# Splitting the gathered rows into two halves, and summing them by two single-pass products

## The reference

```
messages = jnp.einsum('ei,oi->eo', x[col], W) + b
out = jax.ops.segment_sum(messages * agg_weight, row, num_segments=x.shape[0])
x = _layernorm(x + out, axis=-1)
```

## Time and profile before

| | us |
|---|---|
| median of 3 runs (range) | 1298.23 (1295.89 to 1300.33) |
| the profiled execution, its own time | 1291.46 |
| its span, first to last instruction | 1289.7 |
| busy: PE / DVE / ACT / POOL | 962.8 / 756.4 / 650.0 / 577.0 |
| mean granted clock of PE | 0.855 of full |
| sorting part, up to the first step of the second part | about 358 |

### The profile page before, as it was taken

The page is one execution under the profiler, slowest core; times in us unless marked ns, Lnnn a source line. Parts: engine busy times, 40 slices in busy tenths (PEclk is TensorE's granted clock), DMA queues, the critical chain, the costliest instruction groups (busy, mean ns, idle before and its releaser), DMA issues.

```text
span 1289.7 us, 22501 instructions
## 1 busy us (share of the span) xinstructions
PE 962.8 (75%) x7063; PEld 745.4 (58%) x7063; DVE 756.4 (59%) x3474; ACT 650.0 (50%) x1658; POOL 577.0 (45%) x610
## 2 busy tenths in 40 slices
PE   5776877777752676787778777887778777877786
PEld 4543444444432666666667666676667566766676
DVE  7865656566642555566555655565556555655577
ACT  0344444444411464565556555565566555655568
POOL 2344445454454534544454445544544445444520
PEclk9889989889875878898898888877898888887888
DMA  2111111111031444444455445544454445444543
GB/s 68 34 51 34 51 34 51 34 50 48 19 104 41 146 128 139 152 157 138 143 166 155 139 142 151 163 135 138 152 161 141 135 152 167 143 133 143 166 136 136
DMA packets 80818, 147.63 MB, mean 114 GB/s; under 512 B 19152, under 2 KB 20188, under 8 KB 80700
## 3 DMA queue, kind: packets, MB, share of 16 engines
q1 hardware_dynamic: 62076, 117.10, 27.3%
q0 software_dynamic: 18624, 29.08, 8.8%
HBM read 94.19 MB, written 51.93 MB: 113 GB/s over the span
## 4 chain that ended last, share of the span: by engine, by line
PE 42%; DVE 21%; another core or an unknown queue 20%; issue 11%; ACT 5%; DMA 0%; ACTq 0%; POOL 0%; SPq 0%; DVEq 0%; POOLq 0%
PE bank L663 12%; PE bank L681 10%; PE bank L618 8%; DVE stats L946 5%; DVE sel L933 4%; DVE h L940 3%; PE bank L669 3%; DVE mv L952 2%; PE bank L554 2%; PE bank L684 2%; PE bank L573 2%; ACT same_hi L983 2%; PE bank L570 1%; ACT y L1035 1%
## 5 line engine op out<-in xcount | busy, mean ns | idle before, releaser
L507 POOL DMA_INDIRECT xg<-in_x,now x441 | 423.3, 960 | 471.5 <-DVE now L925 338.5
L663 PE MATMUL bank<-sel,xg 128*128 128x308 f32 (+11 forms) x1370 | 359.0, 395 | 80.2 <-issue 69.3
L940 DVE SCALAR_TENSOR_TENSOR h<-bank,aw,xt 128x512 f32<-128x512 f32 x196 | 146.4, 747 | 387.6 <-remote 349.7
L663 PEld LDWEIGHTS bank<-sel,xg 128*128 128x128 f32 x1370 | 264.4, 221 | 142.9 <-issue 114.3
L681 PE MATMUL bank<-wT,aggT 128*128 128x128 f32 x1568 | 263.1, 315 | 103.2 <-issue 69.8
L1035 ACT ACTIVATE y<-h,shift,rstd 128x128 f32<-128x128 f32 x784 | 320.2, 480 | 0.0
L681 PEld LDWEIGHTS bank<-wT,aggT 128*128 128x128 f32 x1568 | 228.0, 219 | 133.7 <-issue 88.3
L1022 ACT COPY aggT<-bank 128x512 f32<-128x512 f32 x196 | 111.9, 571 | 321.0 <-remote 255.7
L470 POOL DMA_INDIRECT place_scratch<-word_col,place_row x141 | 140.6, 997 | 159.7 <-DVE place_row L824 113.6
L946 DVE BATCH_NORM_STATS2 stats<-h 128x6 f32<-128x128 f32 x784 | 169.2, 278 | 0.2
L933 DVE TENSOR_SCALAR sel<-iota_win,now 128x308 f32<-128x308 f32 (+1 forms) x441 | 144.5, 375 | 0.0
(11 more groups left out here) (145 smaller groups left out, 772.5 us busy)
## 6 DMA issues: line engine op xcount, KB each, us to landing
xt<-in_x SPq DMA_DIRECT2D x195, 256.0 KB
out<-y SPq DMA_DIRECT2D x195, 256.0 KB
hi_row<-hi_scratch SPq DMA_DIRECT2D x25, 512.0 KB
xg<-in_x,now POOLq DMA_INDIRECT x441
place_scratch<-word_col,place_row POOLq DMA_INDIRECT x141
place_scratch<-scattered SPq DMA_DIRECT2D x1, 441.0 KB, 6.3
scattered<-place_scratch SPq DMA_DIRECT2D x1, 441.0 KB, 3.2
src_rows<-in_src SPq DMA_DIRECT2D x1, 192.0 KB
```

The costliest lines, as they stand in the source:

```text
L507: nc.gpsimd.indirect_dma_start(out=xg[:, m, k], out_offset=None, in_=x, in_offset=bass.IndirectOffsetOnAxis(ap=now[:, m, k, 0:1], axis=0)) ...
L663: last = nc.tensor.matmul(sums[:, nodes], xg[:, ring, k], sel[:, half, k, cols], start=(i == 0), stop=(i == len(lists) - 1), skip_group_ch ...
L940: V.scalar_tensor_tensor(h[:, u].rearrange("p j d -> p (j d)"), OUT[u % RO][:], aw[:], xt[:, u].rearrange("p j d -> p (j d)"), ALU.mult, A ...
```

## The change

The product of a list is no longer made in float32. The gathered rows are cut by DVE into an upper part, in which the lowest 12 bits of each number are cleared (`cut`), and the rest, `xg - cut` (`xl`). ACT copies the upper part into a buffer of type float32r (`xh`). `xl` and `sel` have this type too. For each product of before, PE makes two, `xh` by `sel` and `xl` by `sel`, into the same sums; float32r is the 32-bit type that PE takes in a single pass. In the trace of before, a float32 product is two instructions, so that the number of instructions on PE stays the same for these sums.

DVE now does two more instructions in each round, one over the 128 to 384 columns of the group's lists on a single source (`cut`), and one on two sources (`xl`), and waits for the gathers there. PE waits no longer for the gathers but for DVE and ACT. ACT has one more copy in each round, ahead of `keep_sums`, whose lag and those of the later stages grow by three. The windows now begin and end at even nodes, so that two of the nine selection matrices are 310 wide. The sorting buffers of the first part have moved into a space that the second part uses again.

```diff
-        sel = sb("sel", [P, 2, LISTS, SW])
+        sel = sb("sel", [P, 2, LISTS, SW], f32r)
+        xh = sb("xh", [P, 2, LISTS, D], f32r)
+        xl = sb("xl", [P, 2, LISTS, D], f32r)
+        cut = sb("cut", [P, 2, LISTS, D])
...
-                    if u % SPAN_G == 0:
-                        pe.wait_ge(s_first[m], 16 * mn + 16)
-                    pe.wait_ge(s_rest[m][u % SPAN_G], (16 * mn + 16) * len([k for k in CLASS[u % SPAN_G] if k]))
+                    pe.wait_ge(s_upper, min(g + 2, GA) if u % SPAN_G == SPAN_G - 1 else g + 1)
+                    pe.wait_ge(s_lower, min(g + 2, GA) if u % SPAN_G == SPAN_G - 1 else g + 1)
...
-                        last = nc.tensor.matmul(sums[:, nodes], xg[:, ring, k], sel[:, half, k, cols],
-                                                start=(i == 0), stop=(i == len(lists) - 1), skip_group_check=True)
+                    for i, (half, k, cols, nodes) in enumerate(lists):
+                        nc.tensor.matmul(sums[:, nodes], xh[:, half, k], sel[:, half, k, cols],
+                                         start=(i == 0), stop=False, skip_group_check=True)
+                        last = nc.tensor.matmul(sums[:, nodes], xl[:, half, k], sel[:, half, k, cols],
+                                                start=False, stop=(i == len(lists) - 1), skip_group_check=True)
...
-                    for k in CLASS[u % SPAN_G]:
+                    mine = CLASS[u % SPAN_G]
+                    lists = slice(mine[0], mine[-1] + 1)
+                    if u % SPAN_G == 0:
+                        dve.wait_ge(s_first[m], 16 * mn + 16)
+                    dve.wait_ge(s_rest[m][u % SPAN_G], (16 * mn + 16) * len([k for k in mine if k]))
+                    V.tensor_scalar(cut[:, m % 2, lists].bitcast(i32), xg[:, m, lists].bitcast(i32), 12, 12, LSR, LSL
+                                    ).then_inc(s_cut, 1)
+                    for k in mine:
                         V.tensor_scalar(sel[:, m % 2, k, 0:WIDTH[k]], iota_win[:, WIN[k]:WIN[k] + WIDTH[k]],
                                         now[:, m, k, 1:2], None, ALU.is_equal).then_inc(s_sel, 1)
+                    dve.wait_ge(s_cut, g + 1)
+                    V.tensor_tensor(xl[:, m % 2, lists], xg[:, m, lists], cut[:, m % 2, lists], ALU.subtract).then_inc(s_lower, 1)
...
+                def keep_upper(g, u, n, period, m, mn):
+                    lists = slice(CLASS[u % SPAN_G][0], CLASS[u % SPAN_G][-1] + 1)
+                    act.wait_ge(s_cut, g + 1)
+                    nc.scalar.copy(xh[:, m % 2, lists], cut[:, m % 2, lists]).then_inc(s_upper, 1)
...
-                rounds([(keep_sums, 0), (spread_of, 3), (normalise, 4)])
+                rounds([(keep_upper, 0), (keep_sums, 3), (spread_of, 6), (normalise, 7)])
```

More of the change, by code:

```diff
@@ L18, in gnn_resnorm_kernel @@
     f32, i32 = mybir.dt.float32, mybir.dt.int32
-    bf16, f16 = mybir.dt.bfloat16, mybir.dt.float16
+    bf16, f16, f32r = mybir.dt.bfloat16, mybir.dt.float16, mybir.dt.float32r
     ALU, ACT, AX = mybir.AluOpType, mybir.ActivationFunctionType, mybir.AxisListType.X
@@ L34, in gnn_resnorm_kernel @@
     FIRST = [-(-SPAN_N * k // LISTS) for k in range(LISTS + 1)]
-    WIN = [(FIRST[k] - TAIL) % GN for k in range(LISTS)]
-    WIDTH = [FIRST[k + 1] - FIRST[k] + TAIL for k in range(LISTS)]
-    SW = max(WIDTH) + max(WIDTH) % 2
+    START = [(FIRST[k] - TAIL) // 2 * 2 for k in range(LISTS + 1)]
+    WIN = [START[k] % GN for k in range(LISTS)]
+    WIDTH = [FIRST[k + 1] + FIRST[k + 1] % 2 - START[k] for k in range(LISTS)]
+    SW = max(WIDTH)
     TAIL_FROM = SPAN_N - LISTS * TAIL
-    CLASS = [[k for k in range(LISTS) if max(FIRST[k] - TAIL, 0) // GN == u] for u in range(SPAN_G)]
+    CLASS = [[k for k in range(LISTS) if max(START[k], 0) // GN == u] for u in range(SPAN_G)]
     PARTS = []
@@ L43, in gnn_resnorm_kernel @@
         for k in range(LISTS + 1):
-            start = FIRST[k] - TAIL
+            start = START[k]
             lo, hi = max(start, u * GN), min(start + WIDTH[k % LISTS], (u + 1) * GN)
@@ L168, in sort_sb @@
                 return sorting.enter_context(nc.sbuf_tensor(name, shape, dt))
+            src_rows = sort_sb("src_rows", [P, KB, P], i32)
+            dst_rows = sort_sb("dst_rows", [P, KB, P], i32)
+            e0 = sort_sb("e0", [P, KB, P], i32)
+            e1 = sort_sb("e1", [P, KB, P], i32)
+            e2 = sort_sb("e2", [P, KB, P], i32)
+            pos = sort_sb("pos", [P, KB, P], i32)
+            chunk = sort_sb("chunk", [P, KB, P], i32)
+            bucket = sort_sb("bucket", [P, KB, P], i32)
+            word1 = sort_sb("word1", [P, KB, P], i32)
+            word2 = sort_sb("word2", [P, KB, P], i32)
             oh_lo = sort_sb("oh_lo", [P, B, BC // 2, LO, 2], bf16)
@@ L269, in gnn_resnorm_kernel @@
         s_sel = sem("s_sel")
+        s_upper = sem("s_upper")
+        s_lower = sem("s_lower")
+        s_cut = sem("s_cut")
         s_agg = sem("s_agg")
@@ L654, in aggregate @@
                     else:
[L655 to L656 removed]
                         pe.wait_ge(s_sel, LISTS * period + LISTS + 1)
                     sums, counts_of = AGG[q], DEG[g // 2 % 2]
[L659 removed]
+                    lists = [((m + k // LISTS) % 2, k % LISTS, slice(lo, hi), slice(at, at + hi - lo))
                              for k, lo, hi, at in parts]
                     at_least(pe, s_aggc, g - 1)
[L662 to L664 removed]
+                    for i, (half, k, cols, nodes) in enumerate(lists):
[3 more added lines that the diff above has]
+                                                start=False, stop=(i == len(lists) - 1), skip_group_check=True)
                     last.then_inc(s_sum, 1)
@@ L667, in aggregate @@
                         at_least(pe, s_degc, g // 2 - 1)
-                    for i, (ring, half, k, cols, nodes) in enumerate(lists):
+                    for i, (half, k, cols, nodes) in enumerate(lists):
                         last = nc.tensor.matmul(counts_of[:, nodes], ones_deg[:, q], selh[:, half, k, cols],
```

14 lines of the change are left out of this document (removed).

## The result

The changed kernel took 1336.87 us (median of 4, 1332.39 to 1338.16), the kernel before 1297.90 (4, 1295.89 to 1300.33). The ratio is 1.0289, 95% interval 1.0252 to 1.0327: slower by 39 us, where 1414, 116 more, was forecast. The sign was right and the size three times too large.

What follows compares the result with a forecast made beforehand. A period was taken as a hole on DVE whose length POOL's gathers set, plus DVE's gapless work. Added work 117 us, less 10 of waits for PE, plus 8 start and 1 end: +116, 1414 us; range 1370 to 1465.

Steps and rivals of the forecast that it cites:

- Added work per period: On DVE: `cut` 0.92, `xl` 1.52 and new waits 0.1 us, together 2.55 us per period, between 2.4 and 3.2.
- The selects kept their rate: On DVE: float32r `sel` costs nothing; rival (6%): nine instructions lose the fast rate, 46 us more, 1460.
- PE's gain is worth nothing: On PE: single-pass products take 2.0 us less per period, but this saves no time in the periods.
- narrow products would cost four passes each: On PE: if the nine products below 256 columns get no benefit, 0.8 us more per period.
- ACT at nothing: On ACT: the added copies, near 1.6 us per period, stay under DVE's time and cost nothing.
- Gathers slowed by the two-port `cut`: On POOL, rival (5%): `cut` holds up gathers, each hole 0.6 us longer, 27 us more, 1441.
- The period is the hole's length plus DVE's work, so nothing hides the added work: On DVE: 8.3 us of hole stays, 10.6 us of work becomes 13.2, so 45.75 periods add 117 us.
- in the hole it didn't run things that were ready: On DVE: the reason given why the hole of 8.3 us would hide none of the added work.
- theory S: The prediction's view, named later: gathers bring every engine to a standstill of fixed length, so all added DVE work is paid.
- the sign itself: Check on the changed profile: the prediction is wrong if DVE's hole shrinks by what was added.
- Start and tail: First rounds, with less done when the long hole begins: 8 us, between 3 and 15; last groups: 1 us.
- the hole takes the work: Rival (9%): DVE does its added 2.5 us inside the 8.3 us hole; only start and tail remain, 1298 to 1308.

Runs made afterwards that it cites:

- a3_f32: Changed kernel with PE's sums made as before, one float32 product, while `cut`, `xl` and `xh` are still made: 1326.09 us, ratio 1.0204 to the kernel before.
- a6: Changed kernel plus a second, unread `cut` and subtraction in the two rounds between `fetch` and the hole: 1263.74 us, ratio 0.9759 to the kernel before.
- a9: Changed kernel with selects made a second time, unread, in the two rounds ahead of the hole (1.6 us): 1331.03 us, ratio 0.9816 to the kernel before.
- a1_pull: Changed kernel with DVE's select of four groups taken together where the hole begins, ahead of `add_x`: 1315.23 us, ratio 1.0154 to the kernel before.
- a7: Changed kernel plus a second, unread `cut` and subtraction in the two rounds behind the hole: 1348.57 us, ratio 1.0382 to the kernel before.
- b4: Kernel before plus unread `cut` and subtraction in the two rounds behind the hole: 1316.64 us (0.9943), on a second chip 1302.07 us (1.0049).

## Why the prediction was right and wrong

- *Added work per period* (0.92 + 1.52 + 0.1 = 2.54, summed as 2.55): right. The pitches give 0.86 for `cut` and 1.47 for `xl`, and no new wait on DVE. The selects kept their rate, 382 ns against 375.
- *PE's gain is worth nothing*: right, and shown by a3_f32. There are as many instructions as before (1370), at 350 and 339 ns in place of 395. At full clock the eight of one group took 1.02 us to the next line (813.57 to 814.59) where they took 1.45 (809.47 to 810.92), and the four groups of a period together 1.6 us less, for the 2.0 that I took; that narrow products would cost four passes each did not come. PE's busy time fell from 962.8 to 932.7 us only.
- *ACT at nothing*: right as far as the runs show. `xh` waits 244.9 us for `cut`, which is DVE's lateness and not its cause. No run takes ACT's copy away and leaves the rest.
- *Gathers slowed by the two-port `cut`* (a rival, by the Trainium skill, "SBUF — State Buffer", section "SBUF: two separate sides"): not seen after, the gathers keep 1.26 us, and two of 441 took over 1.02 us (seven before). In a6, with twice the work there, the second gather of a burst took 1.11 and the fifth 1.48 us (medians) in place of 0.95; in a9, whose filling is selection matrices, the second took 1.15. That is a hint that DVE's work can hold a gather up, and no more.
- *The period is the hole's length plus DVE's work, so nothing hides the added work*: this step failed. It rested on two readings: ready results lay 9.2 us, and DVE was busy for 0.04 us of 8.3. From these I took the hole as a standstill of every engine, of a length that POOL sets. That is theory S, and a1_pull refutes it. The sentence "in the hole it didn't run things that were ready" was wrong: DVE had nothing ready in program order but an `add_x` that waited for PE's signal, and `select` stood behind it. What the gathers set is the hole's end, in three of four periods 12.0 to 12.9 us behind the first of them; DVE sets its start. The term should have been 1.06 us per period and not 2.55, and 1.06 x 45.75 = 48.5; the other mix of kinds leaves the 0.87 measured. The trace of before could have told. In some periods DVE came later to its third `add_x` because the second had waited, as here behind a first gather at 717.34:

```profile
720.87 0.75 DVE L940 SCALAR_TENSOR_TENSOR h<-bank,aw,xt 128x512 f32<-128x512 f32 x1 [1.76 <-PE bank L684]
730.27 0.75 DVE L940 SCALAR_TENSOR_TENSOR h<-bank,aw,xt 128x512 f32<-128x512 f32 x1 [6.42 <-PE bank L684]
735.38 0.17 DVE L925 COPY now<-table 128x18 int32<-128x18 int32 x1
```

  The hole is 6.4 us and not 8.3, it ends at +12.9 all the same, and the period (from the `fetch` at 716.40) is 18.98 us, as the others are. The prediction had named the sign itself: wrong if the hole shrinks by what was added.
- *Start and tail*: predicted 8 and 1 us, measured 5.2 and 2.4. Near enough together.
- The rival that names this, "the hole takes the work", was given 9% and 1298 to 1308, as if it took all or nothing. It takes just what stands between the first gather and the wait.

## To carry over

A wait that begins when the engine gets there and ends at a time set elsewhere absorbs what is added between the event that sets the end and itself, as long as it lasts, and nothing of what is added behind it. Measure both of its edges from the event that sets the end before calling it a fixed cost, and split the added work at that point. Where such a wait lets through a whole number of rounds, small additions can also go with one more, which is worth more here (2 us) than the addition; no sum over durations forecasts that.

## What the runs showed of the hardware

- Gathers of 128 rows by index, nine in a row 1.26 us apart, held up PE: from the sixth on 1.3 to 2.2 of its instructions began per us, on the mean of the bursts of the kernel before, where 7 to 9 do beside the first five. A result that DVE stood waiting for was taken up 9.2 us after its recorded end in the kernel before, one that ACT stood waiting for 4.7 us after in a1_pull. Plain transfers of the same bytes in shorter bursts did none of it (934 us against 1298, PE busy without a gap).
  PE late in a burst of the kernel before (first gather at 827.85):

```profile
834.97 0.42 PE L663 MATMUL bank<-sel,xg 128*128 128x308 f32 x1 [0.61 <-issue]
835.70 0.42 PE L663 MATMUL bank<-sel,xg 128*128 128x308 f32 x1 [0.31 <-issue]
836.41 0.43 PE L663 MATMUL bank<-sel,xg 128*128 128x193 f32 x1 [0.29 <-issue]
837.12 0.32 PE L663 MATMUL bank<-sel,xg 128*128 128x193 f32 x1 [0.28 <-issue]
```

  One begins every 0.71 us, the narrow as the wide, with nothing to wait for that the profile shows. The ends of the holes lie as far apart.
- DVE's own instructions were hardly slowed in that time (a1_pull: matrices of 395 ns for 374).
- In the changed kernel ACT's copy of a sum came at 826.47, its last product having ended by 817.05. ACT waited for `cut` until 825.19, and then still 0.98 us for this result.
- What it is in a gather that holds PE, and why a third round passes early always in a6, in half of a9's periods and in 5 of 44 in the changed kernel, stays open. A count that goes with it: the last gather begins at +10.87, +10.36 and +10.05 us there (medians); in a7, though, it is +10.07 with 20 such periods, and in b4 +10.13 with 23. Open too is why the kernel before runs at 1298 us on some chips and at 1321 to 1387 on others; its patterns of periods are a likely place, but no profile of it was taken there.
